# The triangular product of the edge counts as two matmuls of 64 columns, in a fused graph kernel

## The chip, the cores and the metric

The kernel runs on one core of one Trainium2 chip. The time is the device time of one launch, in microseconds; for the kernel before, three runs are shown, and their median counts. Engines are named as in the profile: PE is TensorE's matmuls, PEld its weight loads, DVE is VectorE, ACT is ScalarE, POOL is GpSimd, and SP is SyncE, which here only issues transfers.

## The reference

A graph of 4096 nodes with 64 features goes through two layers. `adj` is 4096x4096, float32 and sparse.

```python
# layer 0, twice, with weights of its own each time
m = adj @ (x @ W)
gi = m @ wih.T + bih
gh = x @ whh.T + bhh
r, z = sigmoid(i_r + h_r), sigmoid(i_z + h_z)
n = tanh(i_n + r * h_n)
h = relu((1.0 - z) * n + z * x)
...
x = layernorm(x + h2)
# layer 1
support = x @ weight
mask = (adj != 0)
rank = jnp.cumsum(mask, axis=1)
deg = rank[:, -1:]
k = jnp.minimum(deg, 100.)
pos = rank - (deg - k)
w = mask * jnp.where(pos > 0, 0.5 ** (k - pos), 0.0)
out = layernorm(x + w @ support + bias)
```

Layer 1 needs, for every edge, how many edges of its row come after it, since its weight halves with each. This is where the edge counts come from.

## The kernel before

Rows of `adj` are cut into eight chunks of 512. A load (line 400, issued by SP) brings a pair of tiles for one chunk: 128 x 1024 float32, 512 KB, into one of seven slots of `stream`. A pass over a chunk is 16 such pairs. Pass 1 reads all of `adj`; pass 2 reads again what the second product of layer 0 still lacks. A slot is free for the next load when PE has used it (`pair_used`) and, in pass 1, when its mask has been made (`mask_made`, line 903 on DVE).

**The adjacency products** are made by `pair` (line 443). The pair's two tiles go to the two halves of the PSUM rows: tile u writes rows 64u to 64u+63 of the bank, from 64 columns of weights (`state`) and 512 moving columns. So each matmul uses all 128 rows of the array and 64 of its columns. The profile writes this shape as `128*64`; each float32 matmul of the program stands there as two instructions, so that a pair is `x4`. `product1` makes the first product and, for part of the pairs, the second as well (`s_mid`, into `out<-stream,s_mid`).

**The edge counts.** DVE turns the stream into bytes that are 0 or 1 (`mask`), adds them up over the tiles (`sum_quads`, `fold_sums`), and ACT writes the sums as bfloat16 (`to_bf`, line 661, `s_bf_made`). Then `count(b)` (line 484) multiplies them with `tri`, a 128 x 128 triangle of -1 in bfloat16, so that every partition gets the sum over the partitions that come after or before it. Its result in `count_ps`, the bank `out0`, is read by ACT (`start_run`, line 706), which makes the start of the running counts; `guard` and `chain` on DVE go on from there. There are eight counts, one for each chunk. Seven stand in the next chunk's pass, behind pair 5 (`COUNT`), and the last behind the third pair of pass 2 (`n == 2` in `TURN`).

**The order on PE** is written by hand in `pass1` (line 561): behind pair 2 of a chunk the gates of the chunk before (`gates`, lines 503 and 510), behind pair 5 its count, behind pair 8 its node product (`node`, line 526). PE works in this order, and every wait is a semaphore's. Around a count stand two pairs, ahead of it and behind it, of the shape `128*64`. The count is `128*128`.

In pass 2 PE makes the rest of the second product, layer 1's node products and, by `share` (line 532), layer 1's sum over edges with float16 and bfloat16 operands of the shape `128*128`. From 302 us on only layer 1's part is left.

Of the kernel before, what the change touches and what calls it, by code (L numbers as in the profile page):

```python
# [19 lines left out]
D = 64  # L20
# [184 lines left out]
def build(nc, adj_t, x_pairs, w1, consts, bias, out):  # L205
    with ExitStack() as ctx:
        def sb(name, shape, dt):
            return ctx.enter_context(nc.sbuf_tensor(name, shape, dt))

        def sem(name):  # L210
            return ctx.enter_context(nc.semaphore(name))
# [14 lines left out]
        s_bf = sb("s_bf", [P, CW], BF16)  # L226
# [36 lines left out]
        tri = sb("tri", [P, P], BF16)  # L263
# [12 lines left out]
        count_ps, spare_ps = out_ps[0], out_ps[3]  # L276
# [87 lines left out]
        s_bf_made, count_done, start_made = sem("s_bf_made"), sem("count_done"), sem("start_made")  # L364
# [65 lines left out]
        def _(pe):  # L430
# [53 lines left out]
            def count(b):  # L484
                pe.wait_ge(s_bf_made, b + 1)
                if b >= 1:
                    pe.wait_ge(start_made, b)
                nc.tensor.matmul(count_ps[:, :], tri[:, :], s_bf[:, :],  # L488
                                 start=True, stop=True).then_inc(count_done, 1)

            def gates(g):
                layer = g // NCH
# [68 lines left out]
            def pass1(b):  # L561
                for q in range(NP):
# [13 lines left out]
                    if b > 0:  # L576
                        if q == GATES:
                            gates(b - 1)
                        if q == COUNT:
                            count(b - 1)  # L580
                        if q == NODE:
                            node(b - 1)
# [16 lines left out]
            for n, (s, q) in enumerate(TURN):  # L599
                product2(s, q)  # L600
                if n == 1:
                    gates(NCH - 1)
                if n == 2:
                    count(NCH - 1)
                if n == 5:
                    node(NCH - 1)
# [605 lines left out]
```

## Time and profile before

| what | us |
|---|---|
| median of 3 runs | 357.27 |
| lowest and highest run | 357.25, 358.22 |
| span of the profiled execution | 356.2 |
| PE busy (matmuls) | 336.1 (94%) |
| PEld busy | 154.6 (43%) |
| DVE busy | 302.3 (85%) |
| ACT busy | 180.3 (51%) |
| PE's share of the chain that ended last | 80% |
| DMA's share of that chain | 11% |

The profile gives the span of its execution, from the first instruction to the last, and no launch time of its own; the median of the runs is 1.07 us above the span. Matmuls are pipelined: one that is marked 0.59 us long is followed by the next after 0.43 us, so a sum of busy times is not PE's share. Places are best read from the starts of rows and from the chain that ended last. The moved data are 111.10 MB, at a mean of 312 GB/s over the span.

### The profile page before, as it was taken

The page shows a single profiled execution, that of the slowest core. Times are in us where ns is not written, and L with a number is a line of the kernel's source. Part 1 is how long each engine was busy: PE and PEld are TensorE (multiplying, and loading weights), DVE is VectorE, ACT ScalarE, POOL GpSimd, SP SyncE. Part 2 cuts the span into 40 slices and gives each one's busy share as a digit, 9 for nine tenths or more (in the row PEclk, how much of TensorE's full clock was granted, in tenths as well). Part 3 has the DMA queues.
Part 4 walks back from the last instruction along what each step waited for, and adds up shares of the span by engine and source line. Part 5 has one row for each costly group of instructions (what it writes and reads, how often), then busy time and mean ns, then how long its engine had stood idle before and what let it go on. Part 6 is the DMA issues. An engine that isn't in the chain of part 4 may idle for free.

```text
span 356.2 us, 6673 instructions
## 1 busy us (share of the span) xinstructions
PE 336.1 (94%) x2488; PEld 154.6 (43%) x2488; DVE 302.3 (85%) x510; ACT 180.3 (51%) x235; POOL 24.8 (7%) x32
## 2 busy tenths in 40 slices
PE   1999999999999999999999989999999999989992
PEld 1333233333333333333333324544444445879992
DVE  0589989898999999878985666899898999888996
ACT  0202404132041230367466447877895969676993
POOL 2000000000000000000000001202020202022044
PEclk9999999999999999999999999999999999999999
DMA  7999999999998999999998999999999996000012
GB/s 249 413 409 409 409 410 406 410 408 397 407 343 302 411 403 345 310 337 332 309 324 294 379 391 410 344 326 346 341 369 349 395 399 242 17 3 2 2 33 89
DMA packets 32720, 111.10 MB, mean 312 GB/s; under 512 B 3632, under 2 KB 6192, under 8 KB 32688
## 3 DMA queue, kind: packets, MB, share of 16 engines
q1 hardware_dynamic: 31824, 109.20, 81.1%
q10 hardware_dynamic: 864, 1.48, 1.2%
q8 instruction: 20, 0.33, 0.4%
q14 instruction: 12, 0.10, 0.1%
HBM read 109.62 MB, written 1.05 MB: 311 GB/s over the span
## 4 chain that ended last, share of the span: by engine, by line
PE 80%; DMA 11%; DVE 4%; issue 2%; ACT 1%; POOL 1%; POOLq 0%; ACTq 0%; DVEq 0%
PE m_acc L446 42%; PE out L446 15%; DMA stream<-in_adj_t 10%; PE out L555 7%; PE gate_ps L503 4%; PE gate_ps L510 3%; PE gate_ps L555 3%; PE gate_ps L526 2%; PE m_acc L555 2%; DMA w<-in_w 2%; PE gate_ps L438 1%; PE m_acc L478 1%; POOL rstd L843 1%; PE out L488 1%; DVE stream L1155 0%
## 5 line engine op out<-in xcount | busy, mean ns | idle before, releaser
L446 PE MATMUL m_acc<-stream,s_in 128*64 128x512 f32 x512 | 126.0, 607 | 1.6 <-DMA stream<-in_adj_t 1.0
L903 DVE TENSOR_SCALAR codes<-stream 128x1024 uint8<-128x1024 f32 x117 | 76.4, 685 | 3.6 <-DMA stream<-in_adj_t 3.5
L446 PE MATMUL out<-stream,s_mid 128*64 128x512 f32 x272 | 69.3, 595 | 1.5 <-DMA stream<-in_adj_t 1.5
L446 PEld LDWEIGHTS m_acc<-stream,s_in 128*64 128x64 f32 x512 | 33.8, 137 | 65.7 <-issue 52.5
L446 PE MATMUL m_acc<-stream,s_mid 128*64 128x512 f32 x240 | 54.2, 597 | 0.3 <-DMA stream<-in_adj_t 0.3
L843 POOL TENSOR_TENSOR rstd<-var,mhalf 128x4 f32<-128x4 f32 x16 | 23.0, 1436 | 327.7 <-DVE var L1058 327.7
L952 DVE SCALAR_TENSOR_TENSOR codes<-codes,run 128x384 uint32<-128x384 uint32 (+2 forms) x56 | 43.0, 768 | 1.9
L947 DVE TENSOR_TENSOR run<-run,codes 128x768 uint16<-128x768 uint16 (+2 forms) x55 | 41.5, 754 | 1.8
L638 ACT ACTIVATE m_high<-m_acc 64x512 f32<-64x512 f32 x13 | 7.7, 593 | 59.2 <-PE m_acc L446 45.8
L446 PEld LDWEIGHTS out<-stream,s_mid 128*64 128x64 f32 x272 | 19.1, 137 | 40.3 <-issue 39.9
L670 ACT ACTIVATE rz<-gate_ps,b_rz 128x256 f32<-128x256 f32 x32 | 13.4, 469 | 42.8 <-PE gate_ps L510 42.8
L446 PEld LDWEIGHTS m_acc<-stream,s_mid 128*64 128x64 f32 x240 | 16.2, 136 | 32.6 <-issue 31.8
L733 ACT ACTIVATE wexp<-codes,code_bias 128x2048 uint16<-128x2048 uint8 x15 | 29.8, 1994 | 0.1
L733 ACT ACTIVATE codes<-codes,code_bias 128x2048 uint16<-128x2048 uint8 x15 | 29.5, 1987 | 0.0
L920 DVE TENSOR_TENSOR wexp<-wexp,codes 128x2048 uint16<-128x2048 uint16 x16 | 19.6, 1224 | 7.4 <-issue 7.0
L503 PE MATMUL gate_ps<-mx,const 128*64 128x256 f32 x128 | 16.7, 380 | 1.6 <-DVE x1s L1065 1.6
L855 DVE COPY s_in<-gate_ps 128x256 f32<-128x256 f32 x8 | 3.4, 423 | 13.9 <-PE gate_ps L438 13.9
L503 PEld LDWEIGHTS gate_ps<-mx,const 128*64 128x64 f32 x128 | 9.6, 137 | 12.2 <-issue 8.7
L677 ACT ACTIVATE n_g<-t_n,const 128x256 f32<-128x256 f32 x16 | 8.1, 508 | 13.0 <-DVE t_n L984 12.6
L980 DVE SCALAR_TENSOR_TENSOR t_n<-gate_ps,const,rz 128x256 f32<-128x256 f32 x16 | 7.7, 481 | 7.9 <-ACT rz L670 7.7
L1092 DVE TENSOR_SCALAR codes<-codes 128x2048 uint16<-128x2048 uint8 x12 | 14.3, 1218 | 0.0
L693 ACT ACTIVATE mx<-hx 64x256 f32<-64x256 f32 x32 | 13.3, 414 | 0.8
(139 smaller groups left out, 378.6 us busy)
## 6 DMA issues: line engine op xcount, KB each, us to landing
stream<-in_adj_t SPq DMA_DIRECT2D x204, 512.0 KB, 6.1
x_res<-in_x_pairs SPq DMA_DIRECT2D x8, 128.0 KB, 7.2
out_nodes<-stream SPq DMA_DIRECT2D x8, 128.0 KB, 2.0
hx<-in_x_pairs ACTq DMA_DIRECT2D x1, 512.0 KB, 7.2
const<-in_consts ACTq DMA_DIRECT2D x1, 358.0 KB, 6.6
hx<-in_x_pairs ACTq DMA_DIRECT2D x2, 128.0 KB, 6.1
hx<-in_x_pairs ACTq DMA_DIRECT2D x1, 256.0 KB, 8.8
bias_b<-in_bias SPq DMA_DIRECT2D x1, 128.0 KB, 5.4
```

The source lines that it names most:

```text
L446: last = nc.tensor.matmul(to[D * u:D * (u + 1), :], state[:, t * D:(t + 1) * D], stream[:, n % SLOTS, u * CW:(u + 1) * CW], start=start[u] ...
L503: nc.tensor.matmul(to[e * D:(e + 1) * D, 0:HW], w_rz[layer][:, part * D:(part + 1) * D], mx[:, e * HW:(e + 1) * HW], start=True, stop=True)
L555: last = nc.tensor.matmul(end_ps[i][:, t * P:(t + 1) * P], w[:, k * CW + t * P:k * CW + (t + 1) * P], half[:, k, :, :], start=first and t ...
L670: nc.scalar.activation(rz[:, bass.ts(part, HW)], (r_ps, z_ps)[part], ACT.Sigmoid, bias=b_rz[:, 2 * layer + part:2 * layer + part + 1])\
L693: nc.scalar.activation(mx[D:P, e * HW:(e + 1) * HW], state_of(g)[e * D:(e + 1) * D, :], ACT.Copy)\
L733: nc.scalar.activation(weights(j, i).bitcast(U16), block(j, i), ACT.Relu, bias=code_bias[:, :], scale=float(P)).then_inc(by_act, 1)
L843: nc.gpsimd.tensor_tensor(rstd[:, r, :], var[:, r, :], mhalf[:, :], ALU.pow) .then_inc(rstd_made, 1)
L903: nc.vector.tensor_scalar(edges(p // 2, b, 2 * (p % 2), 2), stream[:, n % SLOTS, :], 0.0, None, ALU.not_equal).then_inc(mask_made, 1)
L920: nc.vector.tensor_tensor(to, left, right, ALU.add).then_inc(sum_made, 1)
L947: nc.vector.tensor_tensor(running(n + 1, U16)[:, to], running(n, U16)[:, to], tile_edges(c, k, U16)[:, to], ALU.subtract)\
L952: nc.vector.scalar_tensor_tensor(at, at, EDGE_BIT, running(n, U32)[:, to], ALU.logical_shift_left, ALU.bitwise_or)\
L1092: nc.vector.tensor_scalar(weights(j, i).bitcast(U16), block(j, i), float(P), -float(P * CODE_ZERO), ALU.mult, ALU.add)\
```

## The change

`count` makes the product as two matmuls. Half u takes columns 64u to 64u+63 of `tri` as its weights and writes rows 64u to 64u+63 of `count_ps`, both over the same 512 moving columns of `s_bf`. The semaphore counts on the second half. Operands, results, waits and the place in the order stay.

```diff
                 pe.wait_ge(s_bf_made, b + 1)
                 if b >= 1:
                     pe.wait_ge(start_made, b)
-                nc.tensor.matmul(count_ps[:, :], tri[:, :], s_bf[:, :],
-                                 start=True, stop=True).then_inc(count_done, 1)
+                for u in range(2):
+                    rows = slice(u * D, (u + 1) * D)
+                    last = nc.tensor.matmul(count_ps[rows, :], tri[:, rows], s_bf[:, :],
+                                            start=True, stop=True)
+                last.then_inc(count_done, 1)
```

The order of PE's instructions in the pass over chunk 3, before. `m_acc<-stream,s_in` is the first product, `out<-stream,s_mid` the second, and `x4` here are four matmuls of the program, two pairs.

```order
L503 MATMUL gate_ps<-mx,const 64x256 x4
L510 MATMUL gate_ps<-mx,const 64x256 x4
L446 MATMUL m_acc<-stream,s_in 64x512 x4
L446 MATMUL out<-stream,s_mid 64x512 x2
L446 MATMUL m_acc<-stream,s_in 64x512 x2
L488 MATMUL out<-s_bf,tri 128x512
L446 MATMUL m_acc<-stream,s_in 64x512 x2
L446 MATMUL out<-stream,s_mid 64x512 x2
```

The same place now:

```order
L506 MATMUL gate_ps<-mx,const 64x256 x4
L513 MATMUL gate_ps<-mx,const 64x256 x4
L446 MATMUL m_acc<-stream,s_in 64x512 x4
L446 MATMUL out<-stream,s_mid 64x512 x2
L446 MATMUL m_acc<-stream,s_in 64x512 x2
L490 MATMUL out<-s_bf,tri 64x512 x2
L446 MATMUL m_acc<-stream,s_in 64x512 x2
L446 MATMUL out<-stream,s_mid 64x512 x2
```

One row became two instructions of half its rows, at the same place; the lines below it in the file are three higher. On the other engines nothing changed its place.

## Rows read from the trace of the kernel before

**Rows 1.** The chain that ended last, around the count of chunk 2: start, us, what.

```profile
79.64 0.86 PE out L446 x4
80.49 0.86 PE m_acc L446 x4
81.35 0.32 PE out L488
81.67 1.01 PE m_acc L446 x4
82.68 0.86 PE out L446 x4
```

**Rows 2.** All counts, by line 488: duration ns minimum/median/maximum, first and last start.

```profile
L488 PEld LDWEIGHTS out<-s_bf,tri x8: 95/95/96, 39.0 to 198.4; 128*128 128x128 bf16 x8
L488 PE MATMUL out<-s_bf,tri x8: 389/389/390, 39.0 to 198.4; 128*128 128x512 bf16 x8
```

**Rows 3.** The weight loads around the same count, in order of time.

```profile
80.33 0.14 PEld L446 LDWEIGHTS m_acc<-stream,s_in 128*64 128x64 f32 x2 [0.29 <-issue]
81.28 0.10 PEld L488 LDWEIGHTS out<-s_bf,tri 128*128 128x128 bf16 x1 [0.81 <-issue]
81.60 0.20 PEld L446 LDWEIGHTS m_acc<-stream,s_in 128*64 128x64 f32 x4 [0.23 <-issue]
82.09 0.14 PEld L446 LDWEIGHTS out<-stream,s_mid 128*64 128x64 f32 x2 [0.29 <-issue]
```

**Rows 4.** The matmuls in order of time, float16 of layer 1.

```profile
310.08 1.07 PE L555 MATMUL out<-codes,hx 128*128 128x128 f16 x16
...
311.88 1.95 PE L555 MATMUL out<-codes,wexp 128*128 128x128 f16 x32
```

**Rows 5.** The chain that ended last, around the gates of chunk 2.

```profile
97.16 0.86 PE out L446 x4
98.02 0.86 PE gate_ps L503 x8
```

**Rows 6.** The matmuls in order of time between 82.45 and 82.60, and their mean ns.

```profile
82.08 0.60 PE L446 MATMUL m_acc<-stream,s_in 128*64 128x512 f32 x2
82.51 0.60 PE L446 MATMUL out<-stream,s_mid 128*64 128x512 f32 x2
...
L446 PE MATMUL out<-stream,s_mid 128*64 128x512 f32 x2 | 0.6, 592 | 0.0
```

**Rows 7.** Stretches between counts: length, busy us of the engines, clock, DMA share, GB/s.

```profile
37.90:58.90 21.00, 20.81 (x111) 6.91 (x109) 18.41 (x34) 4.54 (x11) 0.00 (x0) 1.00 1.03 410
58.90:80.10 21.20, 21.04 (x111) 7.21 (x109) 19.13 (x31) 5.98 (x13) 0.00 (x0) 1.00 1.03 409
80.10:101.80 21.70, 21.70 (x115) 7.45 (x113) 19.83 (x34) 4.61 (x10) 0.00 (x0) 1.00 0.99 389
101.80:125.20 23.40, 23.40 (x123) 8.00 (x121) 22.89 (x40) 5.40 (x12) 0.00 (x0) 1.00 0.95 357
125.20:150.40 25.20, 25.20 (x131) 8.60 (x129) 23.55 (x42) 5.89 (x13) 0.00 (x0) 1.00 0.96 354
150.40:176.40 26.00, 26.00 (x135) 8.86 (x133) 22.22 (x40) 16.45 (x23) 0.00 (x0) 1.00 0.94 321
197.20:214.00 16.80, 15.32 (x87) 4.70 (x80) 10.97 (x26) 8.39 (x17) 0.00 (x0) 1.00 1.02 394
```

**Rows 8.** The chain that ended last, where it runs over the stream behind counts 0, 1 and 7.

```profile
37.17 1.03 PE m_acc L446 x4
...
38.22 6.61 DMA stream<-in_adj_t
...
58.77 1.31 PE m_acc L446 x6
...
60.10 6.45 DMA stream<-in_adj_t
...
204.87 8.95 DMA stream<-in_adj_t
...
213.95 1.08 PE out L446 x4
```

**Rows 9.** Who PE waited for from 66.6 to 200 us: total, times, longest.

```profile
PE m_acc L446 <- DMA stream<-in_adj_t: 0.2, 1, 0.2
```

**Rows 10.** DVE behind the count of chunk 2, in order of time.

```profile
86.93 0.68 DVE L963 TENSOR_TENSOR kept<-out,m_high 64x512 f32<-64x512 f32 x1 [1.51 <-ACT m_high L645]
```

**Rows 11.** The loads of the stream: KB each, median us from issue to landing.

```profile
stream<-in_adj_t SPq DMA_DIRECT2D x204, 512.0 KB, 6.1
```

**Rows 12.** DVE in pass 2, in order of time, where it last stands idle before 302 us for longer.

```profile
273.63 0.48 DVE L980 SCALAR_TENSOR_TENSOR t_n<-gate_ps,const,rz 128x256 f32<-128x256 f32 x1 [0.83 <-ACT rz L670]
...
279.64 0.42 DVE L1054 TENSOR_REDUCE stat<-sq 128x4 f32<-128x256 f32 x1 [0.17 <-ACT sq L713]
```

**Rows 13.** The chain that ended last, at the start of the tail.

```profile
302.86 0.86 PE gate_ps L503 x8
...
305.39 1.22 DVE wexp L1092
```

## The prediction

> **What bounds the kernel now.** I read three views, in this order. First the chain that ended last: PE makes 80% of it and the stream of `adj` 11%, so a piece of PE time that goes from the chain is worth its length, unless a wait for the stream stands behind it. Second, the stretches between counts [rows 7]: the granted clock is 1.00, the full 2.4 GHz, in all of them, so the clock plays no part here. Up to 80 us the stream runs at 409 GB/s with its engines all taken; from there to 176 us it falls to 389, 357, 354 and 321 GB/s, while PE is busy through the whole of each stretch. There PE sets the pace. From 197 to 214 us it is the stream again, with 394 GB/s and PE busy 15.32 of 16.80 us. Third, PE's waits: from 66.6 to 200 us it waits for the stream once, 0.2 us at the very start [rows 9]. So the eight counts lie in two kinds of place. Counts 0 and 1 (the first at 39.0 us [rows 2], the second in the stretch from 58.9) have a stretch bound by the stream behind them, and so has count 7 (198.4 us [rows 2]): there the chain runs over a transfer [rows 8]. Counts 2 to 6, one in each stretch between (the last of these from 176.4 us on), lie where only PE counts.
>
> **What a count costs now.** In the chain around count 2 [rows 1] a pair of float32 matmuls takes 0.86 us. The count adds 0.32 us, and the pair behind it takes 1.01 us instead of 0.86. The cost is 0.32 + 0.15 = 0.47 us. All eight counts have the same durations, 389 ns for the matmul and 95 ns for the weights [rows 2], so I take 0.47 for each.
>
> **What it would cost without the change of shape.** How long 512 moving columns of 16-bit values keep the array is read from layer 1: 32 matmuls of 128 columns take 1.95 us and 16 of them 1.07 [rows 4], so 16 more cost 0.88, one costs 0.055, and four, which is 512 columns, 0.22 us. Of the 0.47 us, 0.25 are thus no work: the array runs empty before the count, and again behind it. The weight loads show it [rows 3]. Around the count they start with their matmul, the count's at 81.28 and the pair's at 81.60, while in a run of pairs the next weights are loaded during the matmuls before: four loads within 0.20 us of 81.60 serve two steps, and later steps find theirs in the array.
>
> **The two halves.** Each is an instruction of the shape `128*64`, half u on the same half of the array as tile u of the pairs around it. In a pair the two tiles run side by side: two matmuls of 592 ns stand within 0.60 us, and the next two follow 0.43 us later [rows 6]. The first part of the gates, the same shape with half the columns, shows the same at half the step: eight instructions in 0.86 us [rows 5], four steps of two, 0.215 us each. So I take 0.22 us for both halves of a count, and nothing for the seams. The bounds: below 0.22 it can't be, since the columns have to pass; above, 0.47 if the array still empties for the change from float32 to bfloat16, and 0.94 if each half does so by itself. I take 0.22, since the rows differ from the present pairs in the type alone. **The term: -0.25 us a count.**
>
> One rule speaks against this. The row shows the weights of the next step loaded while matmuls over all 128 rows run (four loads within 0.20 us of 81.60, two of them for the step that follows) [rows 3]. The Trainium skill, page "TensorE: Matmul & The Clock Gate", part 3, "The mechanism", says that a weight load overlaps matmuls in flight only when its group of rows differs. Here all groups of rows are the same, so for halves of columns the trace disagrees with it. It is the mechanism of open loads among the rivals.
>
> **What reaches the end.** For counts 2 to 6 nothing else is on the way: PE does not wait for the stream [rows 9], whose loads are released by PE and come earlier as it does. DVE's work there is tied to PE too: behind count 2 it stands idle for 1.51 us until ACT has read PE's result [rows 10]. Five counts give 5 x 0.25 = 1.25 us. Count 0 and count 1 give nothing: the chain goes from a pair that lies ahead of the count to a load, issued at 38.22 and at 60.10 in a slot which that pair made free, and the load comes at the pace of a full stream of 410 and 409 GB/s [rows 7, 8]. The count is not in this piece at all; PE only waits longer. Count 7 is followed by the load of 204.87, which took 8.95 us in a full stream [rows 8] against 6.1 in the median [rows 11]; it gives nothing, or up to 0.25 where the stream has gaps, which I leave to the range. Past 214 us loads are released by PE, and DVE last starts anew behind results of PE that ACT passes on, 0.83 us idle before 273.63 and 0.17 before 279.64 [rows 12]; then it works through its queue into the tail, which begins with PE's gates at 302.86 and goes on over DVE at 305.39 [rows 13]. So the tail moves as a whole. ACT's `start_run` may read the count a little earlier; it is on no chain. Nothing is put off and no wait is added: the two waits stand on the first half, where they stood on the one matmul.
>
> **The sum.** Against the span of 356.2 us: -1.25, so 354.95. The median of the runs lies 1.07 above that span, and I keep this distance: 357.27 - 1.25 = 356.0 us. A measurement of this kernel can tell about 0.3%, 1.07 us, from no change, so the forecast lies hardly beyond what shows.
>
> **The rivals.**
> *The change does nothing: the seams stay.* The array empties for the change of type, or the halves run one behind the other, 2 x 0.22 = 0.44 us. For it: nowhere in the rows do 16-bit matmuls stand beside float32 ones in one shape, so it is not excluded. Against it: the tiles of a pair run side by side [rows 6]. A count costs 0.44 to 0.47, and the time is 357.2 us. Chance 0.12.
> *Part of it.* Either open loads: weights of 64 columns take 0.14 us [rows 3], and if those of the halves are not hidden, 0.25 - 0.14 = 0.11 is left, 0.55 us in five counts, 356.7. Or DVE holds PE back: from 102 to 125 us it is busy 22.89 of 23.40 us [rows 7], and its masks free the slots. PE that runs 0.5 us ahead may then find a load not there, and counts 3 and 4 give nothing: 3 x 0.25 = 0.75, 356.5. Against it: PE never waited there so far [rows 9]. Chance together 0.13.
> *Slower.* One mechanism: every bfloat16 instruction among float32 ones empties the array for itself, so that two halves pay the seam twice. A count costs 0.94, and five of them on PE's path add 5 x 0.47 = 2.35 us: 359.6. It decides from a cost of 0.68 a count on (0.47 and a fifth of 1.07). Against it: a float32 matmul stands as two instructions, and these follow each other without a seam. Chance 0.05.
> *The forecast* has 0.70.
>
> **How the numbers follow.** In the forecast's case the time lies between 355.2 (all eight counts give 0.25, and 0.1 more) and 356.3 (a part of the gain of one or two counts is taken back by a load that comes too late); about four fifths of it lies beyond the 1.07 us. So faster has 0.55, from 0.70 x 0.79. Slower has 0.05, and with the chance that the seams stay and cost a little more, 0.06. The rest, 0.39, is no difference to be told. The range goes from 355.2 to 357.6: it takes in the forecast, part of it, and no gain with the scatter of the runs, and leaves out the slower case and the forecast's edge.
>
> **What would show it.** In the profile after, the count should stand as two instructions of `128*64` that start some ns apart; the pair behind it takes 0.86 us, not 1.01; and from the end of one pair to the end of the next across the count it is 1.08 us, not 1.33 (0.86 + 0.22 against 0.32 + 1.01). The weights of the count are loaded before its matmul. PE's idle time before the load that now comes at 66.59 grows by the gain of count 1. The gates that now start at 98.02 [rows 5] come 0.25 us earlier than before, and those of each later chunk another 0.25, so that the gates at 302.86 come 1.25 earlier. The prediction is wrong if the pair behind the count keeps its 1.01 us, if PE has new waits between 100 and 200 us, or if the gain is there at 200 us and gone at 300.

## The result, and the profile after

| | before | after |
|---|---|---|
| median, first comparison (4 and 4 runs) | 357.75 us | 355.53 us |
| ratio | | 0.9949 (0.9927 to 0.997) |
| median, second comparison (32 and 12 runs) | 357.20 us | 355.63 us |
| ratio, second comparison | | 0.9965 (0.9951 to 0.998) |
| span of the profiled execution | 356.2 us | 353.8 us |

The change makes the kernel faster by 0.35% (0.20 to 0.49) in the comparison with more runs, and by 0.5% in the first, whose interval holds that value. Of 357.2 us, 0.35% is 1.25 us, the forecast's term, and the interval reaches from 0.7 to 1.75 us. The ratios here and below are the recorded estimates, which are not the quotients of the medians: the medians of the second comparison lie 1.57 us apart (0.44%). Differences between kernels are worked out from the ratios. The two spans lie 2.4 us apart, which is more; where the rest is from is told below.

The chain that ended last, around the count of chunk 2 (start, us, what), for [rows 1]:

```profile
80.67 0.86 PE m_acc L446 x4
81.53 0.22 PE out L490 x2
81.74 0.86 PE m_acc L446 x4
82.60 0.86 PE out L446 x4
```

Both halves together take 0.22 us, where the one matmul took 0.32, and the pair behind them 0.86, where it took 1.01. The counts by their line, for [rows 2]:

```profile
L490 PEld LDWEIGHTS out<-s_bf,tri x16: 110/110/110, 38.6 to 196.8; 128*64 128x64 bf16 x16
L490 PE MATMUL out<-s_bf,tri x16: 379/379/379, 39.1 to 197.2; 128*64 128x512 bf16 x16
```

The matmuls and the weight loads in order of time, for [rows 3] and [rows 6]:

```profile
80.50 1.03 PE L446 MATMUL m_acc<-stream,s_in 128*64 128x512 f32 x4
...
80.93 0.12 PEld L490 LDWEIGHTS out<-s_bf,tri 128*64 128x64 bf16 x2 [0.29 <-issue]
81.36 0.36 PEld L446 LDWEIGHTS m_acc<-stream,s_in 128*64 128x64 f32 x4 [0.31 <-issue]
...
81.36 0.39 PE L490 MATMUL out<-s_bf,tri 128*64 128x512 bf16 x2
81.57 0.60 PE L446 MATMUL m_acc<-stream,s_in 128*64 128x512 f32 x2
```

Two matmuls of 379 ns stand within 0.39 us, so the halves run side by side. Their weights, two loads of 110 ns within 0.12 us, begin at 80.93, 0.43 us ahead of the matmuls at 81.36, while the pair's matmuls of 80.50 run. Each half takes longer to load than the whole did, 110 ns against 95, but under cover. The same place before:

```profile
80.32 1.03 PE L446 MATMUL m_acc<-stream,s_in 128*64 128x512 f32 x4
81.28 0.39 PE L488 MATMUL out<-s_bf,tri 128*128 128x512 bf16 x1
81.60 1.08 PE L446 MATMUL m_acc<-stream,s_in 128*64 128x512 f32 x4
```

The count's load stood at 81.28 with its matmul [rows 3]. The starts show where the 0.25 us were: 0.96 from the pair to the count, now 0.86 (80.50 to 81.36); 0.32 from the count to the next pair, now 0.21; and 0.91 to the pair after that (81.60 to 82.51 [rows 6]), where a pair among pairs takes 0.86.

How this adds up is read from the gates of each chunk, in the chain that ended last (where a row has `x7` or fewer, the asked window ended inside the eight; the start is what counts):

```profile
76.48 0.83 PE gate_ps L506 x7
...
97.93 0.86 PE gate_ps L506 x8
...
121.10 0.86 PE gate_ps L506 x8
...
170.86 0.86 PE gate_ps L506 x8
...
194.88 0.86 PE gate_ps L506 x8
...
300.44 0.86 PE gate_ps L506 x8
```

The same for the kernel before (98.02 stands in [rows 5], which calls them the gates of chunk 2, though by the order of the kernel they are chunk 3's; 302.86 stands in [rows 13]):

```profile
76.31 0.83 PE gate_ps L503 x7
...
121.44 0.86 PE gate_ps L503 x8
...
171.72 0.86 PE gate_ps L503 x8
196.00 0.86 PE gate_ps L503 x8
```

The changed kernel reaches 76 us 0.17 us later, a difference of the first loads. From there each count gives its step: by the clock of the trace the gates stand 0.09 us earlier than before at 98, 0.34 at 121, 0.86 at 171 and 1.12 at 195. Between the gates at 76 and those at 195, with counts 2 to 6 in between, it was 119.69 us and is 118.40, so 1.29 less, 0.26 a count. The gates at 300 come 2.42 us earlier: another 1.3 us went between 195 and 300. From there to the end of the span it is 53.3 us before and 53.4 now.

### The profile page after: what moved, and what is told of

The parts are those of the page before. It is cut to its first block, busy times and chain, and to the rows that moved or that the text cites. A ratio compares the mean times of both kernels' runs of the same rounds, so it can differ in the third digit from the quotient of the medians.

```text
span 353.8 us, 6689 instructions
## 1 busy us (share of the span) xinstructions
PE 333.5 (94%) x2496; PEld 155.2 (44%) x2496; DVE 302.6 (86%) x510; ACT 180.3 (51%) x235; POOL 24.8 (7%) x32
## 4 chain that ended last, share of the span: by engine, by line
PE 82%; DMA 10%; DVE 4%; issue 1%; ACT 1%; POOL 1%; POOLq 0%; ACTq 0%; DVEq 0%
PE m_acc L446 43%; PE out L446 15%; DMA stream<-in_adj_t 8%; PE out L558 7%; PE gate_ps L506 4%; PE gate_ps L558 3%; PE gate_ps L513 3%; PE gate_ps L529 2%; PE m_acc L558 2%; DMA w<-in_w 2%; PE gate_ps L438 1%; PE m_acc L478 1%; POOL rstd L846 1%; DVE stream L1158 0%; PE out L490 0%
```

## The experiments

There are eleven runs, in four groups. The stretch from 76 to 195 us, which several of them are compared by, goes from the start of the gates at about 76 us to that of the gates at about 195, in the chain that ended last. Five counts lie in it, 2 to 6.

### The two kernels once more

No edit. This is for the 1.3 us behind 195 us, and for the scatter.

> The kernel before once more, for a second trace and for the scatter. The change's profiled span is 2.4 us below that of before, and five counts on PE's path explain 1.25. Theory A (the rest is scatter of the stream): this trace has its long gaps between landings at other places than the first one, and its span lies up to 1 us from 356.2. Theory B (the rest is systematic, a gain at the start of pass 2): the stream's stretch from 197 to 214 us looks as in the first trace, with PE waits of about 1.5 us in it, and the span is within 0.3 us of 356.2.

Measured: 357.14 us, ratio 0.9994 (0.9984 to 1.0005), span 355.0. That is 1.2 us from 356.2, a little more than theory A's 1 us and far outside theory B's 0.3.

> The change once more. Both theories: 0.216 us for each count, seam gone. Theory A: the time is 1.2 to 1.6 us below before's (ratio 0.9955 to 0.9966). Theory B: 1.9 to 2.4 us below (ratio 0.993 to 0.9947).

Measured: 355.63 us, ratio 0.9965 (0.9951 to 0.998), span 353.2. The matmuls of the first kernel before in order of time, at the start of pass 2, with what they waited for:

```profile
208.82 0.66 PE L510 MATMUL gate_ps<-mx,const 64*64 64x256 f32 x8
209.41 1.08 PE L446 MATMUL out<-stream,s_mid 128*64 128x512 f32 x4
211.38 1.08 PE L446 MATMUL out<-stream,s_mid 128*64 128x512 f32 x4 [0.89 <-DMA stream<-in_adj_t]
212.67 1.08 PE L446 MATMUL out<-stream,s_mid 128*64 128x512 f32 x4 [0.21 <-DMA stream<-in_adj_t]
213.95 1.08 PE L446 MATMUL out<-stream,s_mid 128*64 128x512 f32 x4 [0.20 <-DMA stream<-in_adj_t]
```

The same kernel, second trace:

```profile
209.18 0.66 PE L510 MATMUL gate_ps<-mx,const 64*64 64x256 f32 x8
209.78 2.79 PE L446 MATMUL out<-stream,s_mid 128*64 128x512 f32 x12
212.73 1.08 PE L446 MATMUL out<-stream,s_mid 128*64 128x512 f32 x4 [0.16 <-DMA stream<-in_adj_t]
```

From the gates to the last of these pairs it is 5.13 us in the first trace (208.82 to 213.95) and 3.55 in the second (209.18 to 212.73), in the same kernel. A load that came late cost the first trace 1.58 us more there. In the second traces, the gates that the tail begins with stand here, in the kernel before:

```profile
301.63 0.86 PE gate_ps L503 x8
```

And in the change:

```profile
299.83 0.86 PE gate_ps L506 x8
```

Before against after, that is 1.80 us, of which 1.28 lie between the gates at 76 and those at 195 (119.68 us in this trace of before, 118.40 in this one of the change). So theory A holds: what the first two spans show beyond the term is to a large part where a late load happened to fall. The ratio of 0.9965 lies at the end of A's range and outside that of B.

### Which counts carry the gain

```diff
-                for u in range(2):
-                    rows = slice(u * D, (u + 1) * D)
+                parts = (slice(0, D), slice(D, P)) if 2 <= b <= 6 else (slice(0, P),)
+                for rows in parts:
                     last = nc.tensor.matmul(count_ps[rows, :], tri[:, rows], s_bf[:, :],
```

> Halves only in counts 2 to 6; counts 0, 1 and 7 as before. Theory A, and the prediction: 1.25 us below before, the same as the whole change within the scatter. Theory B (counts next to the stream's stretches matter as well): 0.5 to 1 us slower than the whole change.

Measured: 356.14 us, ratio 0.9971 (0.9961 to 0.9982), 1.04 us below before. The stretch from 76 to 195 us is 118.61 us long, 1.08 less than before and 0.21 more than in the change, though PE has the same work in it. The 0.21 us are lost at one place: eight matmuls of the first product take 1.93 us from 116.02 on in the chain, where eight take 1.72 elsewhere. What stands behind that is told with the node product below.

The other kernel has `b in (0, 1, 7)` in that place.

> Halves only in counts 0, 1 and 7. The prediction: no gain from 0 and 1, and 0 to 0.25 us from 7, so 0 to 0.25 us below before. Theory B: 0.5 to 1 us below before. If all counts were worth their seam: 0.75.

Measured: 356.81 us, ratio 0.9992 (0.9981 to 1.0003), 0.29 us below before, which is not to be told from none. Its gates stand, in the chain, at:

```profile
76.43 0.86 PE gate_ps L506 x8
...
196.12 0.86 PE gate_ps L506 x8
```

That is 119.69 us, the stretch of the kernel before to the hundredth. The five counts in the middle carry the gain, the three others a small part of it at most; theory B's lower end, 0.5 us for those three, still lies inside the interval, which reaches to 0.68 us. For counts 0 and 1 the traces say more: from the gates at 34 us to those at 76 it is 41.86 and 41.90 us before and 41.83 and 41.93 in the change. The two ratios together, 0.29% and 0.08%, make 0.37%, against 0.35% for the whole.

### The same places with more work

So small a gain is better tested with a larger push the other way. Here the changed kernel makes the halves several times over, which writes the same result again.

```diff
-                for u in range(2):
-                    rows = slice(u * D, (u + 1) * D)
-                    last = nc.tensor.matmul(count_ps[rows, :], tri[:, rows], s_bf[:, :],
-                                            start=True, stop=True)
+                for _ in range(3 if 2 <= b <= 6 else 1):
+                    for u in range(2):
+                        rows = slice(u * D, (u + 1) * D)
+                        last = nc.tensor.matmul(count_ps[rows, :], tri[:, rows], s_bf[:, :],
+                                                start=True, stop=True)
```

> The changed kernel, with the two halves of counts 2 to 6 made three times over (the same result written again). A pair of halves costs 0.216 us, so PE does 0.432 us more at each of five places. Theory A (PE's path there carries all, the ends nothing): 2.16 us slower than the change, 0.9 us slower than before (ratio 1.0025). Rival (the chain has slack there): under 1 us slower than the change.

Measured: 357.1 us, ratio 1.0014 (1.0003 to 1.0025). The chain that ended last:

```profile
76.36 0.86 PE gate_ps L507 x8
...
81.40 0.65 PE out L491 x6
82.05 0.86 PE m_acc L446 x4
...
196.92 0.64 PE gate_ps L507 x5
```

Six halves take 0.65 us, 0.216 for two. The stretch is 120.56 us long, 2.16 more than in the change: the whole of the extra work. The ratio is 0.49% above the change's 0.9965, or 1.75 us, and A's 1.0025 is the upper end of its interval, so some of it may be taken up by the waits for the stream behind 195 us. The rival, under 1 us, is out by the stretch.

The other kernel has `3 if b in (0, 1, 7) else 1`.

> The changed kernel, with the two halves of counts 0, 1 and 7 made three times over. PE does 0.432 us more at each of three places, 1.3 us in all. Theory A (the stream covers counts 0 and 1, and most of 7): 0 to 0.45 us slower than the change (ratio to before 0.9965 to 0.998). Rival (they count like the others): 1.3 us slower than the change (ratio 1.0001).

Measured: 356.14 us, ratio 0.9981 (0.9969 to 0.9993), 0.57 us above the change, of 1.3 us of work. That lies just over the expected 0.45, and the interval holds 0.998, and not the rival's 1.0001. Next, counts 0 and 1 apart from 7, with `range(5 if b < 2 else 1)` and `range(5 if b == 7 else 1)`.

> The changed kernel, with the two halves of counts 0 and 1 made five times over: 0.864 us more of PE work at two places, 1.73 us in all. Prediction's reading (the stream sets the pace there and covers PE's work): under 0.4 us slower than the change (ratio to before 0.9965 to 0.9976), as long as the idle time in front of the loads that come next holds; what it does not hold shows up. Rival (they count like the others): 1.73 us slower than the change (ratio 1.0013).

Measured: 355.29 us, ratio 0.9957 (0.9942 to 0.9972). With 1.73 us more work it is no slower than the change. Its chain:

```profile
37.71 1.29 PE m_acc L446 x6
39.00 1.08 PE out L491 x10
40.08 2.58 PE m_acc L446 x12
```

The ten halves fill 1.08 us, and the chain runs on PE where in the kernel before it ran over a load [rows 8]: the idle time has been filled. Little more came of it: from the gates at 34 us to those at 76 it is 42.05 us, 0.1 to 0.2 more than in the two traces of the change.

> The changed kernel, with the two halves of count 7 made five times over: 0.864 us more at one place. If the stream's stretch behind it covers it: under 0.3 us slower than the change (ratio to before 0.9965 to 0.9973). Rival (its time reaches the end): 0.86 us slower (ratio 0.9989).

Measured: 355.85 us, ratio 0.9972 (0.9959 to 0.9984), 0.25 us above the change with 0.86 us more work. In its chain the stream's piece is still there behind count 7:

```profile
197.61 1.08 PE out L491 x10
...
204.62 8.30 DMA stream<-in_adj_t
```

So count 7 is covered for the most part; the rival's 0.9989 lies outside the interval. Whether 0.25 us of it reach the end or none, the intervals leave open.

### What the seam belongs to

The kernel before, with the full count made twice in a row:

```diff
-                nc.tensor.matmul(count_ps[:, :], tri[:, :], s_bf[:, :],
-                                 start=True, stop=True).then_inc(count_done, 1)
+                for _ in range(2):
+                    last = nc.tensor.matmul(count_ps[:, :], tri[:, :], s_bf[:, :],
+                                            start=True, stop=True)
+                last.then_inc(count_done, 1)
```

> The kernel before, with the full count of 128 columns made twice in a row (the same result). If the seam belongs to the change of shape, the second matmul adds 0.22 us and no seam, and count and pair together take 0.69 us more than a pair instead of 0.47. Rival (each bfloat16 matmul has a seam of its own): 0.94 us.

Its chain around count 2:

```profile
81.41 0.16 issue
81.56 0.38 PE out L489
81.94 1.01 PE m_acc L446 x4
82.95 0.86 PE out L446 x4
```

From the end of one pair (81.41) to the end of the next (82.95) it is 1.54 us, 0.68 more than a pair. The second matmul cost 0.21 us and no seam. The stretch from 76 to 195 us says the same for all five counts: 120.76 us, 1.07 more than before, 0.21 each. The trace has only one of each two matmuls here, and the other's time stands as "issue". Its one run took 358.41 us, with a span of 356.6; a single run gives no ratio.

That the seam comes from 128 columns of weights as such is out by this too: two such matmuls in a row have none. And a seam stands behind the second part of the gates, which has the shape `64*64` and 64 columns of weights: the eight matmuls of the pairs behind it take 1.87 us in the chain (from 77.77 in the kernel before), where eight take 1.72 elsewhere.

Then, in the changed kernel, another product of the program was brought into the pairs' shape. Layer 0's `node` had the shape `64*128`: four matmuls, over 64 rows and 64 moving columns, into two banks. Now half u of the columns of `h` meets all 128 rows of the block-diagonal `w_2`, and ACT's copy reads one bank. A third place, not shown, puts the columns in the old order in that copy.

```diff
-        mid_ps = gate_ps[:, :, 0:2 * D]
+        mid_ps = gate_ps[:, 0, 0:4 * D].rearrange("p (k e d) -> p e k d", k=2, e=2)
...
+                if not layer:
+                    for k in range(2):
+                        for u in range(2):
+                            rows = slice(u * D, (u + 1) * D)
+                            last = nc.tensor.matmul(
+                                gate_ps[rows, 0, k * P:(k + 1) * P],
+                                h[:, k * P + u * D:k * P + (u + 1) * D], rhs[:, :],
+                                start=True, stop=True)
+                    last.then_inc(node_done, 1)
+                    return
...
```

> The changed kernel, and layer 0's node product in the shape of the pairs too: 128 rows, 64 columns, two halves side by side, 128 moving columns, both nodes' halves at once over the block-diagonal weights, all in one bank. If the seam belongs to the change of shape (theory A), a node costs 0.44 to 0.55 us instead of 0.74, its seams are gone, and the five nodes of chunks 2 to 6 give 1.0 to 1.5 us more: 2.2 to 2.7 us below before (ratio 0.9924 to 0.9938). Rival (the count's seam came from its own type or its 128-column weights, not from the shape): a node keeps 0.7 us or more, and nothing is gained over the change.

Measured: 354.24 us, ratio 0.9929 (0.9915 to 0.9943), 2.5 us below before. The matmuls around node 2, in order of time:

```profile
84.15 1.03 PE L446 MATMUL m_acc<-stream,s_in 128*64 128x512 f32 x4
85.01 0.61 PE L529 MATMUL gate_ps<-const,hx 128*64 128x128 f32 x8
85.45 1.89 PE L446 MATMUL m_acc<-stream,s_in 128*64 128x512 f32 x8
```

The same place in the change alone:

```profile
84.15 1.03 PE L446 MATMUL m_acc<-stream,s_in 128*64 128x512 f32 x4
85.10 0.66 PE L529 MATMUL gate_ps<-const,hx 64*128 64x64 f32 x8
85.70 1.51 PE L446 MATMUL m_acc<-stream,s_in 128*64 128x512 f32 x6
```

From the same start the pairs go on at 85.45, not at 85.70. The seam's effect on the weights of the pair behind, another 0.05 us, is gone as well. The node multiplies twice as many elements, half of them zeros, and is faster: the stretches between gates from 121 to 195 us are 0.30 to 0.31 us shorter each than in the change. But the whole stretch from 76 to 195 us is 117.77 us long, 0.63 less than in the change, where five times 0.3 would be 1.5. The trace shows what took the rest:

```profile
116.88 1.08 PE L446 MATMUL m_acc<-stream,s_in 128*64 128x512 f32 x4 [0.68 <-DMA stream<-in_adj_t]
```

PE waits 0.68 us, and the pair behind the wait takes 1.08 us in the chain instead of 0.86. PE is now fast enough to run into a load that isn't there. The chain names the way to it:

```profile
108.53 0.62 DVE codes L915
...
109.58 0.64 SPq L413
...
110.31 6.43 DMA stream<-in_adj_t
...
116.88 1.08 PE m_acc L446 x4
```

A mask of DVE (line 915 here) sets a slot free, SP issues the load into it, then the load of the bias (line 413), then the load that PE will wait for. So this is the rival "DVE holds PE back", between 102 and 125 us where it was looked for, but not DVE alone. The issue of the bias load, which stands in between, takes 0.64 us here and took 0.43 in both traces of the change. And the time of the transfer itself differs: from issue to the last packet's landing this load took 6.43 us here, 5.66 and 6.00 in the two traces of the change (issued at 110.24 and 110.25), and 6.15 in the trace with halves in counts 2 to 6, where the bias load's issue took 0.68, this load was issued at 110.58, and the 0.21 us were lost. No run moved the bias load or the masks, so how much each has in it is not tested.

By the ratios the kernel is 1.3 us below the change, twice what the stretch shows. The interval of such a difference reaches about 0.7 us to either side, and a part of it may lie behind 195 us.

> The kernel before with the node product of layer 0 reshaped in the same way, and the count left at 128 columns. Theory A: the seams of count and node are separate, and the gains add: 1.0 to 1.5 us below before (ratio 0.9958 to 0.9972). Rival as above: no gain.

Measured: 355.64 us, ratio 0.9961 (0.9947 to 0.9974), 1.4 us below before. Its stretch from 76 to 195 us is 118.68 us long, 1.01 less than before, and PE waits at the same place, 0.30 us at 117.50. Here the chain has no DVE ahead of the load: it was issued at 110.85, when PE had freed its slot, and took 6.52 us. The node's reshaping alone is worth about what the count's is, and within the scatter the two add: 0.35% and 0.39% against 0.71% for both.

## Why the prediction was right

**The cost of a count now**, 0.47 us, and **the two halves**, 0.22 us: shown. The halves took 0.216 us, the pair behind them 0.86, and the sum across the count is 1.08 us as named. The step of 0.25 us a count measured 0.26. The bounds above it fall: the change from float32 to bfloat16 in one shape costs nothing to be seen, for the halves follow the pair's matmuls as closely as its own do. What was only inferred from [rows 3], that 0.25 of 0.47 us is the array running empty, is borne out by the full count made twice.

**The rule on weight loads** (the Trainium skill, page "TensorE: Matmul & The Clock Gate", part 3, "The mechanism"), as the prediction gives it from the list there, does not hold for halves of columns: loads over all 128 rows began 0.43 us ahead of their matmuls, while matmuls over the same rows ran. The text above that list leaves room for it, since it also lets a load go ahead when it targets the background weight buffer; the rows do not tell which buffer a load went to.

**What reaches the end.** Counts 2 to 6 give 1.29 us in the trace, and 1.04 by the ratio of their kernel. Counts 0 and 1 give nothing, and can even have 1.73 us of work laid on them. Count 7 was put at nothing, or up to 0.25; the runs hold both. The tail moved as a whole, as said: 53.3 and 53.4 us from its gates to the end.

**The rivals.** That the seams stay, and that each bfloat16 matmul has a seam of its own, are out. That a load comes too late behind a faster PE did not happen in the two traces of the change, as foretold. But it was near: it cost 0.21 us in the one trace with halves in counts 2 to 6 alone, and more with the node's reshaping. "PE never waited there so far" was a weak argument against it, for in the first trace of before that load landed at 116.76, 0.22 us ahead of the pair that uses it (116.98), and a pair that waits starts 0.14 us after the landing (116.74 and 116.88 with the node's reshaping). That the two traces of the change lost nothing there is in part luck.

**The sum.** The second comparison's 1.25 us is the forecast to the hundredth, and that much is luck, for its interval reaches from 0.7 to 1.75 us. The term itself stands on the traces, 1.29 us in five counts. The forecast of 356.0 us is the median before, 357.27, less the term; the two medians measured, 355.53 and 355.63, lie 0.4 to 0.5 us lower. By the medians alone the gain would be 1.57 us in the second comparison and 2.22 in the first. Single runs of the change go from 354.86 to 357.22 us, and none of this is clear of the scatter. One reading beside the sum was wrong: the distance between span and median, 1.07 us, which set the span of one execution against the median of others. It cancels in the time that was forecast. In the twelve profiled executions since, whose own times are shown, the distance is 1.69 to 1.83 us. So the first profiled execution of before took some 357.9 us, 0.6 above that median, and it is the one with the late load at 211 us. That is the larger part of why the first two spans differ by more than the term.

**What would show it.** The gates that stood at 98.02 came 0.09 us earlier by the clock, not 0.25, since the trace began 0.17 us behind. Such places should be compared as stretches, not as points. PE's idle time before the load at 66.59 was to grow by the gain of count 1; it went from 0.17 to 0.20 us. The twelve matmuls ahead of it take 2.98 us instead of 2.79, so PE loses the time at the stream all the same, but for the most part a little earlier. The other signs came: the pair behind the count takes 0.86 us, and PE has no wait between 100 and 200 us.

## What to carry to other kernels

Where matmuls of one shape on the array are broken by a single one of another, look at the distance across it, not at its duration: here 0.25 of 0.47 us was the change of shape, and the cure was to write the odd product in the shape of its neighbours, even at the price of more instructions or of multiplying with zeros. Count what it gives only at places where the chain runs on this engine: three of eight gave next to nothing. When a gain is under half a per cent, compare one stretch of the trace between two fixed points: where no load is late in it, it repeats to about a hundredth of a microsecond, while the spans of the same kernel differed by 1.2 us. And before counting on a further gain at such a place, look how long ahead of its use the next load lands: here one load took 5.66 to 6.52 us from issue to landing in six traces, never more than 0.75 us ahead of the pair that uses it, and a further gain of the same size lost a part of itself to a wait.

## What was not expected

- With the five counts whole, the stretch from 76 to 195 us was 119.69, 119.68 and 119.69 us; in the two traces of the change and in the three with more work at the ends it was 118.40 each time, and 118.61 in the kernel with halves in counts 2 to 6, where a load was late. The spans of the kernel before, 356.2 and 355.0, differ behind 195 us, where the one has a late load that the other has not; why a load lands late there is open.
- A load of 64 bfloat16 columns takes 110 ns and one of 128 takes 95. The halves have twice the loads, each of them longer, and it costs nothing.
- The best version here is the change together with the node's reshaping: 354.24 us, ratio 0.9929.
